# A four-layer graph network: nodes kept in rows of edge order, so that destination rows are loaded and carried along columns

## The reference, cut to what matters

```python
# layer 0, two hops: norm = dinv[src] * w * dinv[dst], self loops included
msg = segment_sum(norm[:, None] * h[src], dst); h = 0.5 * msg + 0.5 * x      # twice
x = layernorm(x + relu(h) @ W.T + b)
# layers 1 and 2, attention with 8 heads
alpha = leaky(a_src . h[src] + a_dst . h[dst] + edge term)
# (layer 1: the edge term is sum(relu(edge_attr @ eW.T + eb) * h[dst]))
attn = softmax of alpha over the edges of one dst
x = layernorm(x + segment_sum(h[src] * attn, dst) + bias)
# layer 3: gather at dst, sum at src
filt = silu(rbf @ Wf1 + bf1) @ Wf2 + bf2
agg = segment_sum(x[dst] * filt, src); h = silu(agg @ Wu1 + bu1) @ Wu2 + bu2
x = layernorm(x + x + batchnorm(h))
```

## Time and profile before

| | |
|---|---|
| median of 3 runs | 8170.37 us (8163.16 to 8176.74) |
| profiled execution, its own time | 8169.49 us |
| its span | 8167.8 us |
| busy: PE, DVE, ACT, POOL | 52%, 65%, 40%, 58% |
| mean DMA rate over the span | 222 GB/s |

### The profile page before, as it was taken

The page is one execution under the profiler, slowest core; times in us unless marked ns, Lnnn a source line. Parts: engine busy times, 40 slices in busy tenths (PEclk is TensorE's granted clock), DMA queues, the critical chain, the costliest instruction groups (busy, mean ns, idle before and its releaser), DMA issues. The chain is left out here.

```text
span 8167.8 us, 82421 instructions
## 1 busy us (share of the span) xinstructions
PE 4280.0 (52%) x18128; PEld 3266.2 (40%) x18128; DVE 5331.3 (65%) x16616; ACT 3287.2 (40%) x8834; POOL 4767.5 (58%) x4730
## 2 busy tenths in 40 slices
PE   7800000799963333488511111003877877999854
PEld 4400000688852222366411111002555554888733
DVE  7856677677767777799744446997444444455577
ACT  4567300688851111388500001443222222444499
POOL 7777677544447777566577776666777777000000
PEclk9955555899975555699855555556888887999955
DMA  9299899777767677799755556886555554666699
GB/s 273 7 279 311 291 301 299 234 243 243 243 194 222 221 222 224 231 357 357 258 179 179 177 178 187 270 270 182 83 83 84 84 84 77 197 203 203 203 361 348
DMA packets 1128113, 1764.26 MB, mean 216 GB/s; under 512 B 247612, under 2 KB 606500, under 8 KB 1127626
## 3 DMA queue, kind: packets, MB, share of 16 engines
q1 hardware_dynamic: 641162, 903.37, 33.4%
q0 software_dynamic: 238720, 537.64, 26.8%
q10 hardware_dynamic: 247744, 318.00, 11.2%
HBM read 968.89 MB, written 840.95 MB: 222 GB/s over the span
## 5 line engine op out<-in xcount | busy, mean ns | idle before, releaser
L673 POOL DMA_INDIRECT st<-S,last_i x1176 | 1152.3, 980 | 872.8 <-DVE yt L714 364.7
L903 POOL DMA_INDIRECT rows<-T,src_i x784 | 749.4, 956 | 238.9 <-issue 238.9
L616 ACT ACTIVATE xo<-z,shift,rsd 128x256 f32<-128x256 f32 x1568 | 849.9, 593 | 0.5 <-issue 0.2
L1123 POOL DMA_INDIRECT A<-comb,ai x392 | 628.8, 1604 | 161.7 <-issue 135.7
L916 PE MATMUL psE<-encs,attr 4*128 4x256 f32 x784 | 369.7, 648 | 620.0 <-DMA attr<-in_attr3T 617.8
L933 ACT ACTIVATE psX<-diff 128x40 f32<-128x40 f32 x196 | 40.7, 208 | 1592.4 <-DVE diff L989 1592.4
L916 PE MATMUL psE<-fes,attr 64*128 64x8 f32 x784 | 183.3, 360 | 804.4 <-DMA attr<-in_attr64T 802.1
L1137 PE MATMUL psH<-rbf,wf1s 20*128 20x256 f32 x784 | 264.7, 464 | 603.3 <-DMA rbf<-in_rbfT 603.3
L1195 DVE TENSOR_SCALAR eq<-psI,src_f 128x128 f32<-128x128 f32 x392 | 136.8, 349 | 668.9 <-DMA A<-comb,ai 597.5
L565 PE MATMUL psC<-sums,chain 128*128 128x256 f32 x4 | 2.4, 700 | 1082.6 <-PEq L454 1082.6
L588 DVE BATCH_NORM_STATS2 row_stats<-z 128x6 f32<-128x256 f32 x1568 | 561.3, 400 | 0.1
(11 more groups left out here) (241 smaller groups left out, 14232.2 us busy)
## 6 DMA issues: line engine op xcount, KB each, us to landing
X<-xo ACTq DMA_DIRECT2D x588, 256.0 KB
xt<-X SPq DMA_DIRECT2D x588, 256.0 KB
S<-sums SPq DMA_DIRECT2D x196, 544.0 KB, 3.1
S<-sums SPq DMA_DIRECT2D x392, 256.0 KB, 3.9
A<-zero SPq DMA_DIRECT2D x196, 512.0 KB, 4.6
T<-tt ACTq DMA_DIRECT2D x196, 280.0 KB
T<-tt ACTq DMA_DIRECT2D x196, 272.0 KB
XT<-in_x SPq DMA_DIRECT2D x1, 50176.0 KB, 169.4
```

The costliest lines, as they stand in the source:

```text
L616: ins = e.activation(y[s][:, k, :], z[s][:, k, :], ACT.Identity, bias=shift[s][:, k, :], scale=rsd[s][:, k, :])
L673: e.indirect_dma_start(st[s][:, k, :], None, sums_table, bass.IndirectOffsetOnAxis(ap=last_i[:, c:c + 1], axis=0))\
L903: e.indirect_dma_start(rows[s][:, k, :], None, table, bass.IndirectOffsetOnAxis(ap=src_i[:, c:c + 1], axis=0))\
L1123: e.indirect_dma_start(A[k], bass.IndirectOffsetOnAxis(ap=ai[s][:, k, :], axis=0), comb[s][:, k, :], None, compute_op=ALU.add).then_inc(si ...
```

## The change

Each node gets one row of its own in the order of edges. A node with edges takes the row of its first edge (for the tables X1, T1) or of its last (X2, T2, ET, X3); a node without edges takes one of the rows that are left. Setup pairs the k-th node without edges with the k-th row that is left: `compress` packs the flagged columns of each partition to the left in 10 rounds of shifting, matrix products bring the right stretches of another partition's list, and `expand` spreads the list again, in 10 rounds; each is done twice. The results are index lists: `index_i` (source rows, three variants, stored beside the degree in XT), `input_i`, `turn_i` and `node_i`.

The node stages then load S plainly, and gather the node's features instead: `x` with `input_i`, X1 with `turn_i`; `layer_nodes(2)` gathers nothing. A row that is not a node's last edge must not take the sum: `cut` zeroes its weight. The attention stages load the destination's row plainly. Layer 1 zeroes it off the first edges on ACT (`cut_rows`) and carries it to the right on DVE (`spread_rows`); layer 2 loads all of ET once and spreads it in 8 scans. The filter stage walks from the right, and does the same with X3; POOL issues only the adds there, each waiting for the last one into its own table. `finish_nodes` gathers X3 with `node_i`. Hops and filter walk the columns from right to left, so that the full sum of a hop stands at the first edge. The functions `locate`, `own` and `join` of setup, the new column order of the hops, the index arithmetic, and the host's extra input `dst_prev` are left out below.

```diff
+                        def compress(j, flag, count):
+                            to, tmp_ = listed[j], other[:, 0, :]
...
+                            for b in reversed(range(BITS)):
+                                link(e.tensor_scalar(bit[:], rem[:], float(2 ** b), None, ALU.is_ge))
+                                e.scalar_tensor_tensor(rev[:], bit[:], float(2 ** (BITS - 1 - b)), rev[:], ALU.mult, ALU.add)
+                                link(e.scalar_tensor_tensor(rem[:], bit[:], -float(2 ** b), rem[:], ALU.mult, ALU.add))
+                            link(e.tensor_scalar(rev[:], rev[:], CODE, 1.0, ALU.mult, ALU.add))
+                            link(e.tensor_tensor(rev[:], rev[:], cols[:], ALU.add))
+                            link(e.memset(to[:, 0:C], 0.0))
+                            link(e.tensor_tensor(to[:, C:W], rev[:], flag[:], ALU.mult))
+                            for b in range(BITS):
+                                d, top = 2 ** b, CODE * 2 ** (BITS - 1 - b)
+                                a, z = (to[:], tmp_) if b % 2 == 0 else (tmp_, to[:])
+                                e.tensor_scalar(moved[:, 0, :], a, top, 0.0, ALU.subtract, ALU.max)
+                                link(e.scalar_tensor_tensor(z, a, top, a, ALU.is_lt, ALU.mult))
+                                link(e.tensor_tensor(z[:, 0:W - d], z[:, 0:W - d], moved[:, 0, d:W], ALU.add))
...
+                        def expand(j, turn):
+                            link(e.tensor_tensor(shift[:], listed[j][:], pos[:], ALU.subtract))
...
+                                    part_ = codes[:, v, h * C:(h + 1) * C]
+                                    link(e.tensor_tensor(part_, psL[v][h][:, 0:C], shift[:, h * C:(h + 1) * C], ALU.add))
+                                    link(e.tensor_tensor(part_, part_, there[:, h * C:(h + 1) * C], ALU.mult))
+                            e.sem_inc(taken, 1)
+                            for b in reversed(range(BITS)):
+                                d, top = 2 ** b, CODE * 2 ** b
+                                a, z = (codes, other) if b % 2 else (other, codes)
+                                e.tensor_scalar(moved[:], a[:], top, 0.0, ALU.subtract, ALU.max)
+                                link(e.scalar_tensor_tensor(z[:], a[:], top, a[:], ALU.is_lt, ALU.mult))
+                                if d < W:
+                                    link(e.tensor_tensor(z[:, :, d:W], z[:, :, d:W], moved[:, :, 0:W - d], ALU.add))
+                            link(e.tensor_scalar(ids[:], codes[:, 1, C:W], float(C), -float(C + 1), ALU.mult, ALU.add))
+                            link(e.tensor_tensor(ids[:], ids[:], codes[:, 0, C:W], ALU.add))
...
+                    @block.gpsimd
+                    def _(e):
+                        e.wait_ge(placed, 16)
+                        e.indirect_dma_start(brow[:, 0, :], None, XT, bass.IndirectOffsetOnAxis(ap=dst_i[:, 0:1], axis=0)).then_inc(bounded, 16)
+                        e.indirect_dma_start(brow[:, 1, :], None, XT, bass.IndirectOffsetOnAxis(ap=dst_i[:, C - 1:C], axis=0)).then_inc(bounded, 16)
 
                     @block.sync
                     def _(e):
-                        e.wait_ge(clamped, TABLE)
+                        e.wait_ge(tabled, 1)
                         e.wait_ge(widened, 16)
                         e.dma_start(nodes(XT)[:, :, D:XW], degs[:]).then_inc(placed, 16)
...
+            xin, at_i = ((x.rearrange("p c d -> (p c) d"), input_i), (X1, turn_i), (X2, None))[layer]
...
 
                         unrolled(R, NS, [(load, 0)])
 
-                    @block.gpsimd
...
+                        def cut(i, s):
+                            hold(e, *done(st_["weighed"], i, s))
+                            own = islast[:, bass.ds(i * (G * NS) + s * G, G)].rearrange("p (g h) -> p g h", h=1).to_broadcast([P, G, H])
+                            e.tensor_tensor(den[s], den[s], own, ALU.mult).then_inc(signal(st_["cut"], s), 1)
...
+                table, at_i = (T1, index_i[:, 1, :]) if layer == 1 else (T2, index_i[:, 2, :])
...
-                        written(N, NS, [(stage, 0), (store, 2), (empty, 2)])
+                        def take(i, s):
+                            hold(e, *done(spread_, i, s, NS - 1))
+                            e.dma_start(rowsd[s][:], nodes(T1)[:, bass.ds((i * NS + s) * G, G), :]).then_inc(signal(taken, s), 16)
+
+                        if layer == 2:
+                            e.dma_start(own_t[:], nodes(ET)).then_inc(owned, 16)
+                        written(N, NS, ([(take, 0)] if layer == 1 else []) + [(stage, 0), (store, 2), (empty, 2)])
                         for sem, value in total_of(stored, N):
                             e.wait_ge(sem, value)
                         e.wait_ge(emptied, 16 * N)
@@ -898,11 +1122,13 @@
                             hold(e, *done(summed, i, s, NS))
...
                                 c = (i * NS + s) * G + k
-                                e.indirect_dma_start(rowsd[s][:, k, :], None, dtable, bass.IndirectOffsetOnAxis(ap=dst_i[:, c:c + 1], axis=0))\
+                                e.indirect_dma_start(rows[s][:, k, :], None, table, bass.IndirectOffsetOnAxis(ap=at_i[:, c:c + 1], axis=0))\
                                     .then_inc(signal(gathered, s), 16)
-                                e.indirect_dma_start(rows[s][:, k, :], None, table, bass.IndirectOffsetOnAxis(ap=src_i[:, c:c + 1], axis=0))\
-                                    .then_inc(signal(gathered, s), 16)
-
...
+                        def cut_rows(i, s):
+                            hold(e, *done(taken, i, s))
+                            for k in range(G):
+                                ins = e.activation(rowsd[s][:, k, :], rowsd[s][:, k, :], ACT.Copy, scale=isfirst[:, bass.ds((i * NS + s) * G + k, 1)])
+                            ins.then_inc(signal(cut, s), 1)
...
+                            e.wait_ge(ends, 16)
+                            e.wait_ge(owned, 16)
+                            e.tensor_tensor(own_t[:], own_t[:], islast[:].rearrange("p (c h) -> p c h", h=1).to_broadcast([P, C, H]), ALU.mult)\
+                                .then_inc(csteps, 1)
+                            e.wait_ge(csteps, 1)
+                            e.scalar_tensor_tensor(own_t[:, C - 1, :], tail[:], notlast[:, C - 1:C], own_t[:, C - 1, :], ALU.mult, ALU.add)\
+                                .then_inc(csteps, 1)
+                            e.wait_ge(csteps, 2)
+                            for h in range(H):
+                                ins = e.tensor_tensor_scan(all_t[:, ::-1, h], follows[:, ::-1], own_t[:, ::-1, h], 0.0, ALU.mult, ALU.add)
+                            ins.then_inc(csteps, 1)
...
+                        def spread_rows(i, s):
+                            hold(e, *done(cut, i, s))
+                            for k in range(G):
+                                c = (i * NS + s) * G + k
+                                last = rowsd[s][:, k - 1, :] if k else rowsd[(s - 1) % NS][:, G - 1, :] if i + s else head[:]
+                                ins = e.scalar_tensor_tensor(rowsd[s][:, k, :], last, notfirst[:, c:c + 1], rowsd[s][:, k, :], ALU.mult, ALU.add)
+                                if k < G - 1:
+                                    ins.then_inc(csteps, 1)
+                                    e.wait_ge(csteps, (i * NS + s) * (G - 1) + k + 1)
...
-                        written(N, NS, [(score, 0), (add, 1)])
+                        written(N, NS, ([(spread_rows, 0)] if layer == 1 else []) + [(score, 0), (add, 1)])
...
                             hold(e, *done(hidden, i, s, NS))
                             e.dma_start(rbf[s][:], rbfT[:, c, :]).then_inc(signal(attred, s), 16)
 
-                        unrolled(R, NS, [(stage, 0)])
+                        def take(i, s):
+                            c = bass.ds(C - (i * NS + s + 1) * G, G)
+                            hold(e, *done(message, i, s, NS))
+                            hold(e, *done(spread_, i, s, NS - 1))
+                            e.dma_start(rows[s][:], nodes(X3)[:, c, :]).then_inc(signal(taken, s), 16)
+
+                        unrolled(R, NS, [(take, 0), (stage, 0)])
...
                     def _(e):
-                        def gather(i, s):
-                            hold(e, *done(message, i, s, NS))
-                            for k in range(G):
-                                c = i * (G * NS) + s * G + k
-                                e.indirect_dma_start(rows[s][:, k, :], None, X3, bass.IndirectOffsetOnAxis(ap=dst_i[:, c:c + 1], axis=0))\
-                                    .then_inc(signal(gathered, s), 16)
-
                         def add(i, s):
                             hold(e, *done(copied, i, s))
-                            hold(e, *done(added, i, s, 1))
                             for k in range(G):
+                                hold(e, *done(added[k], i, s, 1))
```

(24 more changed lines are left out.)

386 lines of the change are left out of this document (289 added, 97 removed).

## The result

The changed kernel takes 7847.2 us, the median of 4 runs (7844.8 to 7854.0), beside 8166.8 for the kernel before (4 runs, 8162.2 to 8176.7). The ratio is 0.961, with a 95% interval from 0.9592 to 0.9625: faster by 3.9%. The profiled execution took 7853.95 us, its span is 7852.0. The forecast was 7820, its range 7690 to 7990.

What follows compares the result with a forecast made beforehand. Stages were bound separately: both attention stages and the filter by POOL, later node stages by DVE, the last by ACT and DMA. 208 + 15 - 315 + 33 + 43 - 413 + 80 = -349, from 8169.5 to 7820 us, range 7690 to 7990.

Steps and rivals of the forecast that it cites:

- Setup: Setup stage: the added index work is a chain on DVE with no other engine working; +208 us, 190 to 230.
- attention layer 1: First attention stage: POOL's gathers halve but DVE takes over, 10.15 us a step against 10.05; +15 us.
- attention layer 2: Second attention stage: the loop through SP's stores and attribute loads sets 6.65 us a step; -315 us.
- SP's order does not hold attention layer 2: Rival, attention layer 2: attributes land sooner, DVE sets 5.3 us a step; -133 us more, 7690 in all; chance 0.13.
- The node stages: layer_nodes(1) and (2): DVE is the limit and `cut` adds 0.22 us a step; +33 and +43 us, gather changes free.
- Filter: Filter stage: POOL keeps only the adds, landing loop 4.05 us a step, 4.4 taken with coupling; -413 us.
- three engines within 0.2 us: Filter stage: POOL 4.05, PE 4.15 to 4.3, DVE 4.2 us a step, so 4.4 taken for their coupling.
- no engine waits long: Sign to look for in the filter stage: no engine waits long and the clock is near full.
- The rival with a mixed clock: Filter stage: PE stays at clock 0.83, 5.1 us a step, stage 1035, kernel 7958 us; chance 0.16.
- Last stage: Last stage: 392 gathers on POOL at 1.29 us each set its length, 526 us against 446.5; +80 us.
- POOL locked out by DVE: Rival: two-source DVE instructions stop POOL's descriptor work, 8.0 us a step in attention layer 2; +132, 7952 us; chance 0.07.
- the sum of -349: Whole kernel: 208 + 15 - 315 + 33 + 43 - 413 + 80 = -349 us, from 8169.5 to 7820.

Runs made afterwards that it cites:

- e7: Changed kernel with X1 loaded plainly by SP in layer_nodes(1) instead of 392 gathers on POOL; that stage 647.9 us against 650.4.
- e2: Changed kernel with the filter's adds going round four tables instead of two, the further two not summed; filter stage 815.4 us against 965.3 and 952.9.
- e6: Changed kernel with stores one step later, two tables A cleared in setup, three add tables, `cut` replaced by a floor; 7932.4 us, 0.972 of the kernel before.
- e3: Changed kernel with all the filter's adds into one table, each waiting for the one before; filter stage 1713.6 us.
- e5: Changed kernel with tables A cleared in setup's first part, not during attention; attention layer 2 fell by 91 us, layer 1 by 26, setup took 422 more.
- e8: e6 with one table's clearing in setup's second part and the other's at the start of its third; 7789.5 us, 0.907 of the kernel before.
- c_before: The kernel before, unedited, run again last for the lengths of its stages; 8588.5 us.
- c_after_2: The changed kernel, unedited, run again in the third set of runs; 8054.8 us, 0.938 of the kernel before.
- c_after: The changed kernel, unedited, run again in the second set of runs; 7842.3 us, 0.961 of the kernel before.
- e1: Changed kernel with SP's stores of S and zeros one step later in both attention stages; layer 2 gave 61 us, layer 1 24 us.

## Why the prediction was right, point by point

**Setup, attention layer 1, attention layer 2** came out as worked, to 1, 0 and 2 us. For layer 2 the runs confirm the mechanism too, from both ends: with SP's stores one step later two of three steps run at DVE's 5.3 us, with a shorter queue ahead of the attributes a step is 0.93 us shorter, and with both every step is at 5.3. That is also the rival "SP's order does not hold attention layer 2" refuted. Setup's parts came out one by one. For layer 1 two loops close to each other were forecast, DVE 9.95 to 10.0 and SP's path at 9.75, and 10.15 taken; measured 10.19 with both and 9.98 with SP's path relieved. The 0.15 for two close loops was a guess that came out.

**The node stages**: the step "0.22 a step, 196 x 0.22 = 43" measured 43 to 44 in layer 2. In layer 1 the 33 were 25. That a gather of X1 is free there was shown by e7.

**Filter, the one step that failed**: "each table's add must land first, 3.9 median: 4.05 a step". The landing time was right, the loop around it was not: 4.32 us with one add at a time, 4.8 with two tables. That is 0.4 a step above the 4.4 taken, 80 us, less 10 at the start. The forecast also saw three engines within 0.2 us and added 0.2 for their coupling. The runs show none: with the landing loop out of the way the step is 4.0 to 4.1, below what I had for PE (4.15 to 4.3) and DVE (4.2). Those two values were too high, and hid part of the miss: with right ones I would have forecast some 4.2 a step. The upper bound, 5.2 a step, held. The forecast's sign, that no engine waits long, did not: POOL waited 227 us for landings. The rival with a mixed clock (0.83, 5.1 a step) did not come: the granted clock was 0.96 at 4.8 a step, 0.99 at 4.0 to 4.1 (e2, e6) and 0.74 where PE waited most (e3).

**Last stage**: 1.25 us a gather (946 ns and 0.30) where 1.29 was taken from the hops. I had carried over the slower row, 1010 ns, for its dense DVE; it was as quick as in attention. The prediction's reading of that row, contention with DVE's sums, does not follow from how busy DVE is: it was busy 355 of 506 us here and 367 of 531 in the second hop of the kernel before, the same 70%, and a gather took 946 ns against 1010. What makes the hop's gather slower stays open.

**POOL locked out by DVE** did not come. The Trainium skill (GPSIMD Engine Reference, Specifications) has GpSimd's SBUF interfaces shared with VectorE. In attention layer 1, with DVE busy 934 of 1038 us, a gather took 981 ns on average against 956 before: the first of each four 1.09 us, the other three 0.945. In layer 2 it took 956. So what this case could show of that contention is at most 0.025 us a gather.

Against the sum of -349 the span came out 33 us too long: the filter 69 too dear, the last stage 20, the node stages 12 and the rest 4 cheaper. That the whole is nearer than the filter alone is luck: half of its miss was made up by terms that have nothing to do with it.

## What to carry to other kernels

Where instructions go round a loop through a DMA that must land, price the loop from issue to issue in a trace, not by the landing time: it was 0.4 to 0.9 us more than that here, and a third destination table took the loop away for 45 us elsewhere. When one engine is relieved, look at the queue of SyncE next: a small load behind a large store waits for its data as well as for its turn, and both can be moved. And busy time is no bound on the step: that of a PE that waits in every step was too high (4.39 us where 4.05 did), that of a DVE in a chain of short dependent instructions too low (9.5 where the chain takes 9.95).

## What the runs showed of the hardware

A list of large stores holds its engine. In e5 and e6 98 stores of 1 MB stood on SP's list with nothing waiting for them, and SP was busy issuing them: in e6 39 of them, from 300.4 us on, took it 120.3 us, 3.1 each, the time of the transfer; a part of the program that ends with all engines drained could not end. On SP where it had nothing else to do the same stores cost nothing (e8: setup 627.7 us).

The sets of runs differ. The expectations put this down to the chip; but the first set, with the longer times, and the second, without, have the same chip number on record, so that is not shown. The last run was the kernel before, for its stages.

> The kernel before, for the lengths of its stages. In two of the three sets of runs so far its time was 8589 to 8631 us in place of 8165, and the changed kernel's 8055 in place of 7842; there the changed kernel's hops took 60 and 40 us more, its last stage 92 and nothing else over 10. If a gather costs more there wherever it is the limit, the kernel before loses the same 100 us in its hops and the other 330 in its attention stages and its filter, which POOL's gathers held; its last stage, without gathers, stays at 446. If this set of runs is like the second one, all stages are as in the profile shown.

It took 8588.5 us. Hops 583 and 568 (before: 522.5 and 531.5), the last stage 443.7, filter 1302.5, and the attention stages:

```profile
2471.30:3640.10 1168.80, 377.18 (x816) 250.26 (x816) 735.42 (x1590) 143.79 (x395) 751.49 (x786) 0.50 0.60 188
4273.90:5462.80 1188.90, 190.76 (x816) 180.76 (x816) 493.06 (x1391) 38.90 (x200) 748.23 (x786) 0.50 0.48 148
```

Here 312 of the 419 us sit in the attention stages, as expected, and none in the filter, which was not. POOL's busy time is what it was the earlier trace rows. What is new are pauses, as in this timeline of c_before:

```profile
3001.85 1.24 DVE L1001 TENSOR_TENSOR rows<-rows,psX 128x1056 f32<-128x1056 f32 x1
3002.28 0.94 POOL L903 DMA_INDIRECT rows<-T,src_i  x1 [0.30 <-issue]
...
3007.56 0.43 DVE L1003 TENSOR_TENSOR sums<-psD,rows 128x264 f32<-128x264 f32 x1 [4.46 <-DMA xt<-in_x]
```

L1003 needs only what DVE itself wrote, and comes 4.46 us late; the DMA that the row names belongs to another stage. What stops DVE there stays open. The attention stages of the changed kernel, with half the gathers, show nothing of it in their lengths (1039.4 and 702.0 us in c_after_2, 1039.8 and 699.2 in c_after), and so its gain was 6.2% in such a set and 3.9% in the others. But its layer 2 has slack, a wait for PE in 88 of its 98 steps. Where that was taken away the pauses show again: e8, the same code as e6 there, took 644.8 us in place of 566.1, with the same median step of 5.30 us and 19 of 97 steps above 6.9, and e1, with only the stores moved, took 639.4. So e1's 61 us are not what the order of SP is worth by itself: in sets with the longer times, removing the zeros as well (e8) gained nothing more.
